# Six banks for a first down projection, and five orders changed at the end of self-attention

## What is computed

```
x = layernorm(x + self_attention(x))            # 16 heads of 32, window mask, wq wk wv wo 512x512
x = layernorm(x + cross_attention(x, context))  # 16 heads of 128, rmsnorm of q and k with gains
x = layernorm(x + moe(x))

def moe(x):
    y, g = split(x @ shared_gw.T)
    shared = silu(g) * y @ shared_dw.T
    scores = sigmoid(x @ gate_w.T)                 # 8 experts, the best 2 of scores + bias
    w = scores[best 2] / sum
    for e in experts:
        g_e, u_e = split(x @ up_w[e].T)
        out = out + (silu(g_e) * u_e) @ down_w[e].T * w_e
    return shared + out
```

## Time and profile before

| | |
|---|---|
| median of 3 runs | 1051.37 us (1051.21 to 1051.67) |
| profiled execution | 1057.8 us, span 1056.1 us |
| mean granted TensorE clock | 0.995 of full speed |
| TensorE busy | 1024.9 us, 97% |
| VectorE, ScalarE, GpSimd busy | 703.9, 524.3, 531.4 us |
| DMA | 153.45 MB, mean 145 GB/s |

### The profile page before, as it was taken

The page is one execution under the profiler, slowest core; times in us unless marked ns, Lnnn a source line. Parts: engine busy times, 40 slices in busy tenths (PEclk is TensorE's granted clock), DMA queues, the critical chain, the costliest instruction groups (busy, mean ns, idle before and its releaser), DMA issues.

```text
span 1056.1 us, 20141 instructions
## 1 busy us (share of the span) xinstructions
PE 1024.9 (97%) x7000; PEld 908.3 (86%) x7000; DVE 703.9 (67%) x1454; ACT 524.3 (50%) x1033; POOL 531.4 (50%) x515
## 2 busy tenths in 40 slices
PE   8999989999999999999999999999999899999997
PEld 8866568999999999999999999999887787787785
DVE  4378866776866767767767767767776454545447
ACT  5355546555545545545545555455543245565520
POOL 1257857745535534534534634634572734544543
PEclk9999999999999999999999999999999999999999
DMA  8100104324333223223233223224210869999833
GB/s 282 76 31 2 60 27 153 148 109 160 111 108 112 104 106 112 103 106 112 100 108 113 101 106 111 102 107 151 93 66 1 328 233 383 385 380 385 307 113 117
DMA packets 45272, 153.45 MB, mean 145 GB/s; under 512 B 3768, under 2 KB 4792, under 8 KB 42144
## 3 DMA queue, kind: packets, MB, share of 16 engines
q1 hardware_dynamic: 42976, 145.38, 38.4%
q0 software_dynamic: 2240, 7.34, 2.1%
HBM read 130.04 MB, written 22.66 MB: 145 GB/s over the span
## 4 chain that ended last, share of the span: by engine, by line
PE 73%; POOL 4%; DVE 4%; issue 3%; ACT 2%; another core or an unknown queue 0%; POOLq 0%; DVEq 0%; ACTq 0%
PE xa_y_ps L86 6%; PE xa_y_ps L88 5%; PE xa_y_ps L87 5%; PE ex_raw_ey_ps L2142 5%; PE ex_raw_gu_ps L86 4%; PE ex_raw_gu_ps L88 4%; PE ex_raw_gu_ps L87 4%; PE xa_c_ps L1930 4%; PE xa_c_ps L1926 4%; PE xa_c_ps L1925 3%; PE xa_turn_ps L2007 3%; PE xa_turn_ps L1963 3%; PE front_k_ps L86 3%; PE front_k_ps L88 3%; PE front_k_ps L87 3%
## 5 line engine op out<-in xcount | busy, mean ns | idle before, releaser
L1271 POOL TENSOR_TENSOR xa_probs<-xa_probs,xa_inv_sum 112x750 f32<-112x750 f32 x63 | 97.7, 1551 | 75.8 <-DVE xa_inv_sum L1598 75.8
L1547 DVE TENSOR_TENSOR xa_kT_lo<-xa_turn_ps,xa_kT_hi 128x750 fp32r<-128x750 f32 x63 | 59.2, 940 | 99.9 <-ACT xa_kT_hi L1359 99.8
L1256 POOL TENSOR_TENSOR k_ms<-k_ss,sum_eps 125x6 f32<-125x6 f32 x63 | 12.5, 198 | 210.9 <-DVE k_ss L1563 210.9
L1925 PE MATMUL xa_c_ps<-xa_probsT_hi,xa_nat 125*128 125x224 f32 x384 | 92.8, 275 | 2.7 <-ACT xa_probsT_hi L1375 2.7
L1926 PE MATMUL xa_c_ps<-xa_probsT_hi,xa_nat 125*128 125x224 f32 x384 | 92.8, 276 | 0.0
L1375 ACT CAST xa_probsT_hi<-xa_turn_ps 125x672 fp32r<-125x672 f32 x62 | 44.7, 720 | 86.6 <-PE xa_turn_ps L2007 86.6
L1259 POOL TENSOR_TENSOR k_inv<-k_ms,neg_half 125x6 f32<-125x6 f32 x63 | 83.4, 1324 | 8.3 <-POOL k_ms L1256 6.6
L1381 ACT ACTIVATE xa_probs<-xa_scores_ps,xa_bias,xa_q_scale 112x375 f32<-112x375 f32 x126 | 82.6, 662 | 5.9 <-DVE xa_bias L1573 4.7
L1925 PEld LDWEIGHTS xa_c_ps<-xa_probsT_hi,xa_nat 125*128 125x128 f32 x384 | 73.8, 192 | 3.6 <-issue 3.1
L1926 PEld LDWEIGHTS xa_c_ps<-xa_probsT_hi,xa_nat 125*128 125x128 f32 x384 | 73.9, 192 | 0.5
L86 PE MATMUL front_k_ps<-land_xa_wk_hi,land_xa_ctx 128*125 128x256 f32 x252 | 71.4, 283 | 1.6 <-DVE front_k_hat L1590 1.2
(11 more groups left out here) (393 smaller groups left out, 3495.4 us busy)
## 6 DMA issues: line engine op xcount, KB each, us to landing
xa_nat<-ctx_split SPq DMA_DIRECT2D x56, 750.0 KB
ex_raw_raw<-in_w_units SPq DMA_DIRECT2D x15, 1408.0 KB, 8.3
ex_raw_raw<-in_w_units SPq DMA_DIRECT2D x15, 768.0 KB
land_ex_raw<-in_w_units SPq DMA_DIRECT2D x8, 1408.0 KB, 7.9
land_ex_raw<-in_w_units SPq DMA_DIRECT2D x8, 768.0 KB, 8.0
ctx_split<-xa_nat SPq DMA_DIRECT2D x8, 750.0 KB
sorted_x<-ex_raw_y_sb SPq DMA_DIRECT2D x7, 768.0 KB, 10.5
ex_raw_x_nat<-sorted_x SPq DMA_DIRECT2D x21, 256.0 KB, 8.4
```

What stands on the lines that cost most here:

```text
L1271: pool.tensor_tensor(probs[0:T, u % 2], probs[0:T, u % 2], inv_sum[0:T, u % 2, :].unsqueeze(2).broadcast_to([T, 2, KV]), ALU.mult).then_in ...
L1547: dve.tensor_tensor(kT_lo[:, :, 0:KV], turn_ps[:, :, 0:KV], kT_hi[:, :, 0:KV].bitcast(F32), ALU.subtract).then_inc(sem["kT_lo_done"], 1)
L1925: pe.matmul(c_view[:, c], nat[0:KT, u % 2, 0, at], probsT_hi[0:KT, :, cols], start=(t == 0), stop=False)
```

## The change

1. The low part of wo, one 128x512 operation of VectorE in each of the slots 3 to 6, is halved: VectorE keeps columns 0 to 255, GpSimd does the others behind `masked` of that slot.
2. The low part of wq (GpSimd, 128x1024) moves from behind slot 23 to the tail, behind `power(TILES - 2)`.
3. The low parts of contexts 4 and 5 move from VectorE's slots 28 and 30 to GpSimd's tail, beside those of 6 and 7.
4. Output tile 5 is summed in `proj_ps` and tile 4 turned in `y_ps`, with the waits that go with it.
5. In the tail TensorE makes the first queries ahead of the last output product, and VectorE the normalised keys ahead of the last addition and the low part of the first queries ahead of the last normalisation.
6. In dense unit A the down tiles use six banks: the two of `ey_ps`, then the four of `gu_ps`, and `ey_ps` again for tile 6.

```diff
@@ GpSimd, behind masked(s) and in the tail
+                if s in wo_slots:
+                    q = wo_slots[s]
+                    wait(pool, "wo_hi_done", q + 1)
+                    pool.tensor_tensor(wo_part(qk_lo, q)[:, D // 2:D], wo_raw[:, q, D // 2:D], wo_part(qk_hi, q)[:, D // 2:D].bitcast(F32),
+                                       ALU.subtract).then_inc(sem["wo_lo_half"], 1)
                 if s == 19:
                     weights_low("wk")
-                if s == 23:
-                    weights_low("wq")
...
             power(TILES - 2)
+            weights_low("wq")
...
-            for k in (6, 7):
+            for k in (4, 5, 6, 7):
@@ VectorE
-                    dve.tensor_tensor(wo_part(qk_lo, q), wo_raw[:, q, :], wo_part(qk_hi, q).bitcast(F32),
+                    dve.tensor_tensor(wo_part(qk_lo, q)[:, 0:D // 2], wo_raw[:, q, 0:D // 2], wo_part(qk_hi, q)[:, 0:D // 2].bitcast(F32),
...
-                if s - 1 in ctx_slots:
+                if s - 1 in ctx_slots and ctx_slots[s - 1] < HALF:
...
-            add_output(TILES - 1)
-            means(TILES - 1)
             dve.wait_ge(first["kinv_done"], 1)
...
-            normalise(TILES - 1)
+            add_output(TILES - 1)
+            means(TILES - 1)
             dve.wait_ge(first["gain_ready"], 1)
             queries_low(0)
+            normalise(TILES - 1)
@@ TensorE, self-attention
+            def wait_for_bank(t):
+
+                wait(pe, "proj_copied", len(PROJ))
+                if t == TILES - 2:
+                    wait(pe, "v_copied", B)
+                    wait(pe, "turn_lo", t - 1)
+                elif t == TILES - 1:
+                    wait(pe, "y_added", t - 1)
+                    wait(pe, "turn_lo", t - 1)
+                else:
+                    wait(pe, "y_added", t)
...
+            first_queries(0)
             output_product(N - 1)
-            first_queries(0)
-            turn(pe, TILES - 2)
+            turn_tile(TILES - 2)
@@ expert stage
+        first_down_ps = [ey_ps[:, 0], ey_ps[:, 1], gu_ps[:, 0, 0], gu_ps[:, 0, 1], gu_ps[:, 1, 0], gu_ps[:, 1, 1], ey_ps[:, 0]]
...
+                bank = first_down_ps[t] if base == 0 else ey_ps[:, n % 2, :]
+                dve.tensor_tensor(resid[:, t, :], resid[:, t, :], bank, ALU.add).then_inc(xs["y_taken"], 1)
...
-                if n >= 2:
+                if base == 0:
+                    bank = first_down_ps[t]
+                    if t in (2, 4):
+                        pe.wait_ge(xs["mul_done"], UPS - 2 + t // 2)
+                    if t == TILES - 1:
+                        pe.wait_ge(xs["y_taken"], 1)
+                else:
+                    bank = ey_ps[:, n % 2, :]
                     pe.wait_ge(xs["y_taken"], n - 1)
...
                 pe.wait_ge(xs["mul_done"], n - 1)
+                if j < 2:
+                    pe.wait_ge(xs["y_taken"], 2 * j + 4)
```

More of the change, by code:

```diff
@@ L255, in self_attention @@
         st, mv, rstd, half = env["ln_stats"], env["ln_mv"], env["ln_rstd"], env["neg_half"]
-        turn, turn_high, turn_low = turn_stages(nc, env, sem, sem["ln_done"], [proj_ps])
+        turn, turn_high, turn_low = turn_stages(nc, env, sem, sem["ln_done"], [proj_ps] * 4 + [y_ps, proj_ps, proj_ps])
         block = es.enter_context(nc.Block())
@@ L318, in tile_cols, with tile_bank @@
             return slice(at, at + P)
+        def tile_bank(t):
+            return proj_ps if t == TILES - 2 else y_ps
         def ends_tile(u):
@@ L790, in turn_probs, with turn_tile @@
                 mm.then_inc(sem["probsT_ready"], 1)
+            def wait_for_bank(t):
[8 more added lines that the diff above has]
+                    wait(pe, "y_added", t)
+            def turn_tile(t):
+                wait(pe, "turn_lo", t)
+                if t == TILES - 3:
+                    wait(pe, "y_added", t + 1)
+                turn(pe, t)
             def output_product(u):
@@ L796, in output_product @@
                 wait(pe, "wo_lo_done", q + 1)
+                wait(pe, "wo_lo_half", q + 1)
                 wait(pe, "oT_lo_done", u + 1)
                 if q == 0:
-                    wait(pe, "y_added", t)
-                    wait(pe, "proj_copied", len(PROJ))
-                three_products(pe, y_ps[:], oT_hi[:, q, tile_cols(t)], oT_lo[:, q, tile_cols(t)], wo_part(qk_hi, q),
+                    wait_for_bank(t)
+                three_products(pe, tile_bank(t)[:], oT_hi[:, q, tile_cols(t)], oT_lo[:, q, tile_cols(t)], wo_part(qk_hi, q),
                                wo_part(qk_lo, q), q == 0, q == QUADS - 1).then_inc(sem["y_ready"], 1)
@@ L808, in first_output_product @@
                 wait(pe, "wo_lo_done", q + 1)
+                wait(pe, "wo_lo_half", q + 1)
                 wait(pe, "oT_lo_done", u + 1)
                 if q == 0:
-                    wait(pe, "y_added", t)
-                    wait(pe, "proj_copied", len(PROJ))
-                pe.matmul(y_ps[:], oT_hi[:, q, tile_cols(t)], wo_part(qk_hi, q), start=(q == 0), stop=False)
+                    wait_for_bank(t)
+                pe.matmul(tile_bank(t)[:], oT_hi[:, q, tile_cols(t)], wo_part(qk_hi, q), start=(q == 0), stop=False)
             def rest_of_output_product(u):
@@ L868, in _ @@
                     wait(pe, "v_copied", min(t + 5, B))
-                    turn(pe, t)
+                    turn_tile(t)
                 for n in range(*PROJ_SLOTS.get(s, (0, 0))):
@@ L893, in _ @@
             outputs(N - 1)
+            first_queries(0)
             output_product(N - 1)
-            first_queries(0)
-            turn(pe, TILES - 2)
+            turn_tile(TILES - 2)
             first_queries(1)
-            turn(pe, TILES - 1)
+            turn_tile(TILES - 1)
             pe.wait_ge(first["khat_done"], 2)
@@ L2095, in dense_down @@
                     w = slice(c * D, (c + 1) * D)
-                    mm = three_products(pe, ey_ps[:, n % 2, :], h_hi[0:m, c, cols], h_lo[0:m, c, cols],
+                    mm = three_products(pe, bank, h_hi[0:m, c, cols], h_lo[0:m, c, cols],
                                         down_hi[0:m, w], down_lo[0:m, w], c == 0, c == HC - 1)
```

10 lines of the change are left out of this document (5 added, 5 removed).

## The result

| | before | changed |
|---|---|---|
| median of 5 runs each, side by side | 1051.21 us (1050.62 to 1051.67) | 1056.15 us (1054.98 to 1057.07) |
| ratio | | 1.0037, 95% interval 1.0026 to 1.0049 |
| profiled execution | 1057.8 us, span 1056.1 | 1057.03 us, span 1055.3 |

The changed kernel is slower by about 0.4%: a loss of 3.9 us (by the ratio) to 4.9 us (by the medians) stands where a gain of 4.2 was forecast. The two traces don't show it: by their spans the changed kernel is 0.8 us faster. The reason is that the profiled execution of before was an odd one, 6.4 us over its median, and that excess sat mostly where the prediction took its largest term from.

The account below looks back on a forecast made before the run. TensorE, busy 97% of the span, bounds the kernel, so edits pay only at its idle, half-clock or barrier stretches. -5.38 + 1.29 - 1.03 + 0.93 = -4.19, so 1051.37 - 4.2 = 1047.2 us; range 1044.4 to 1050.0.

Parts of the forecast that it names:

- Six banks: First down projection, expert stage: TensorE's 3.57 us idle and the slow clock after it (the hole) go, gaining 5.38 us.
- I take the difference as it is and put it on the median: Whole kernel: -4.2 us, priced on a profiled execution 6.4 us over the median, applied to the median 1051.37.
- Low parts of wo: Self-attention slots 3 to 6: GpSimd's half, about 0.6 us, waits for ScalarE's rounding and delays scaling, costing 1.29 us.
- The upper bound of 2: Self-attention, wo's low parts: the most they would cost, +2 us, if GpSimd's half takes 0.9 us.
- The rival of hidden halves: Self-attention: ScalarE's rounding comes early enough and wo's halves hide, giving -1.4 us there, kernel 1044.5; chance 0.17.
- Low part of wq: Self-attention, slot 23 to tail: TensorE's 0.83 us wait goes, with 0.2 of the next scaling's lateness, gaining 1.03 us.
- Contexts, second bank, tail order: End of self-attention: four context parts on GpSimd end the stage at the barrier, costing 0.93 us.
- clock at the barrier: Start of cross-attention: after some 4.6 us idle the clock falls, losing up to 1.65 us, kernel 1048.2 to 1048.9; chance 0.15.

Follow-up runs that it names:

- no_halves_no_contexts: Changed kernel with wo's low parts whole on VectorE and contexts 4 and 5 back in its slots: 1049.94 us against 1056.9; run again (_2) 1049.4, ratio 0.9978.
- banks_and_wq: Kernel before with only the six banks and wq's low part in the tail: 1050.19 us against 1051.84, ratio 0.9984.
- after_again: The changed kernel, unaltered, run again in another batch: 1055.78 us against 1051.42 for the kernel before, ratio 1.0039.
- before_again: The kernel before, unaltered, run again for its trace, in a batch where before took 1056.9 us; the traced execution took 1056.15 us.

## Why the prediction was wrong

*Six banks, -5.38.* The arithmetic of the new rows held to 0.03 us. What failed is the step "I take the difference as it is and put it on the median": the profiled execution was 6.4 us longer than the runs, with two stretches of low clock to see in its own windows, and one of them was this term. In executions like the timed ones the banks give 0.8 us by the traces (13.81 - 13.02) and 0.6 to 0.7 by the medians, which the intervals don't tell from nothing; 4.55 of the 5.38 belong to an execution with the hole. There the term fits: no_halves_no_contexts gained 7.0 us in the batch with it and 1.9 in the one without, by the medians, 5.1 apart; the banks alone never ran in a batch with the hole. The row itself spoke: VectorE's wait ended on "remote", within 0.04 us of SyncE's loads (842.20 and 842.24), although its semaphore is that of the first tile's scatter alone.

*Low parts of wo, +1.29.* The mechanism was right in place and order, the waits 0.83, 0.48 and 1.50 at the three turns that it worked out. Two sizes were not. The operation takes 0.98 and not 0.6, most likely since it starts just behind VectorE's half; the prediction's own chain, with 0.38 more in each of three slots, gives 1.89 + 3 x 0.38 = 3.03 at the third turn, and 3.11 was measured. So by that chain the term should have been 1.29 + 1.14 = 2.4. The clock, which this term put at nothing, falls behind the waits; what is left of the 3.67 in the trace, about 1.2, is put down to it here and not measured apart. Measured in all 3.4 to 4.5. The upper bound of 2 was no bound: it took 0.9 for the operation and no clock. The rival of hidden halves fell.

*Low part of wq, -1.03.* Right: 1.02 by the traces.

*Contexts, second bank, tail order, +0.93.* GpSimd does end the stage, and TensorE waits 4.3 us, forecast as 4.6. With wq's -1.03 the prediction had cross-attention start 0.10 us earlier than before; without the halves it starts 105.36 - 104.98 = 0.38 later. The larger miss is the clock behind it, 1.33 us: the rival "clock at the barrier", which came true within its price of up to 1.65 and which the sum put at nothing. It should have stood in the forecast: the prediction had seen 0.50 after 3.57 us of idle in this trace. As an edit the contexts cost 2.6 to 3.0. Second bank and order together: no_halves_no_contexts_2 lies 0.6 us (by the ratios, 0.9978 and 0.9984, between batches) under banks_and_wq, within both intervals, and 0.18 by the table, so that a gain in the times isn't shown.

*The sum.* By parts, from traces without the hole: -0.8 (banks), -1.0 (wq), -0.2 (bank and order), +2.9 (contexts with the clock), +3.7 (halves): +4.6; measured +3.9 by the ratio and +4.9 by the medians, +4.1 and +4.4 in after_again. Of the 8 to 9 us between forecast and result 4.6 are the banks, 2.4 the halves and 1.8 the barrier and its clock.

*What stays open.* Why the first addition is late in some batches. The wait before it may end with the scatter's semaphore; but ScalarE's silu ahead of it is late too, by 0.5 us (834.24 - 833.51 against 0.20) in before_again and by 1.2 in before, and waits for nothing of the scatter. Late instructions would explain both, a late DMA completion only the addition. No run tells them apart.

## What to carry to other kernels

If the profiled execution is longer than the median of the runs by more than the term you are about to price, find that excess in the trace first; low-clock windows and waits that end on "remote" or "issue" are where it hides, and a term read there may not be in the timed runs at all. An operation given to an idle engine costs by its place: ahead of an operation that the slots' chain needs, it brings its own producer into the chain. Count traces from a row ahead of the edit, not from their start: here 0.3 to 0.4 us of the differences at the barrier had nothing to do with the edits. Price stalls of TensorE together with the clock behind them.
